# Attention message passing on one core: two tiles for the drained product bank, earlier spreading scans, and a later second widening

## The reference

```python
def _egat_layer(nf, ef, src, dst, W_ni, W_nj, W_fij, W_node, attn, bias):
    f_out = nf @ W_ni [src] + nf @ W_nj [dst] + ef @ W_fij + bias
    f_out = leaky_relu(f_out, 0.2).reshape(-1, H, D)
    e = einsum('ehd,hd->eh', f_out, attn)
    a = exp(e - segment_max(e, dst)[dst])
    a = a / segment_sum(a, dst)[dst]
    h = (nf @ W_node).reshape(-1, H, D)
    return segment_sum(h[src] * a[:, :, None], dst), f_out
for l in range(3):
    nfh, efh = _egat_layer(nf, ef, src, dst, ...)
    nf, ef = nfh.mean(axis=1), efh.mean(axis=1)
return x + nf
```

## Time and profile before

| | |
|---|---|
| median of 2 runs | 3717.05 us (3715.75 to 3718.35) |
| the profiled execution | 3716.28 us, its span 3714.5 us |
| TensorE busy | 2692.3 us, 72% |
| VectorE busy | 2424.4 us, 65% |
| GpSimd busy | 1891.6 us, 51% |
| ScalarE busy | 1634.7 us, 44% |
| mean granted TensorE clock | 0.777 of 2.4 GHz |

### The profile page before, as it was taken

How to read it: one execution, slowest core, us unless ns; L and a number is a source line. 1 busy time by engine, 2 the same in 40 slices (tenths; PEclk the granted TensorE clock), 3 DMA queues, 4 the chain that set the end, 5 groups by cost and what they waited for, 6 DMA issues and landing times.

```text
span 3714.5 us, 54737 instructions
## 1 busy us (share of the span) xinstructions
PE 2692.3 (72%) x18232; PEld 2153.1 (58%) x18259; DVE 2424.4 (65%) x5843; ACT 1634.7 (44%) x4133; POOL 1891.6 (51%) x1987
## 2 busy tenths in 40 slices
PE   3477777768677458777777777856777787777885
PEld 2465656656565256566666656536666666666653
DVE  6376767767768536676676767753667576676775
ACT  0144544544445315454454545532444444444453
POOL 5544554554553266455554545446555454554543
PEclk8787777777879778787777878868777777777776
DMA  6244334434342334343434433233343333433322
GB/s 218 86 122 137 120 122 144 128 126 133 122 130 88 121 107 119 115 137 114 147 120 134 126 115 122 98 107 110 100 121 119 112 108 105 123 114 114 95 81 84
DMA packets 149064, 440.48 MB, mean 119 GB/s; under 512 B 40892, under 2 KB 80672, under 8 KB 129977
## 3 DMA queue, kind: packets, MB, share of 16 engines
q1 hardware_dynamic: 82746, 385.31, 29.4%
q0 software_dynamic: 63200, 36.75, 7.1%
q10 hardware_dynamic: 2838, 14.91, 1.0%
HBM read 191.89 MB, written 244.95 MB: 118 GB/s over the span
## 4 chain that ended last, share of the span: by engine, by line
DVE 36%; PE 36%; issue 13%; ACT 9%; DMA 4%; POOL 2%; DVEq 0%; ACTq 0%; SPq 0%; POOLq 0%
DVE U L1465 15%; PE pick_ps L732 14%; PE f_ps L764 11%; PE f_ps L773 5%; DVE U L1450 4%; ACT f_low L919 4%; DVE rows L1386 4%; PE xT_ps L754 4%; DVE lr L1397 4%; DVE rows L1491 3%; ACT xT L910 2%; DMA z<-hot_tab 1%; ACT pick_sb L973 1%; DVE z L1477 1%; DVE mx_sc L1421 1%
## 5 line engine op out<-in xcount | busy, mean ns | idle before, releaser
L615 POOL DMA_INDIRECT rows<-nf_tab,src_sb x1815 | 1721.8, 949 | 1505.0 <-PE xT_ps L754 669.6
L732 PE MATMUL pick_ps<-nf_part,z 125*128 125x160 bf16 x9045 | 926.1, 270 | 578.9 <-ACT pick_sb L973 446.4
L732 PEld LDWEIGHTS pick_ps<-nf_part,z 125*128 125x128 bf16 x9045 | 835.1, 115 | 624.4 <-issue 459.9
L1397 DVE TENSOR_TENSOR lr<-f_ps,f_low 128x512 f32<-128x512 f32 x606 | 413.3, 682 | 930.7 <-ACT f_low L919 930.5
L773 PEld LDWEIGHTS f_ps<-w_out,lr 128*128 128x128 f32 x4836 | 721.4, 215 | 396.4 <-issue 296.7
L764 PE MATMUL f_ps<-xT,w_edge 97*128 97x512 f32 x1212 | 804.5, 752 | 70.2 <-ACT ef_new L941 47.2
L1465 DVE TENSOR_TENSOR_SCAN U<-wide_ps,U 128x272 f32<-128x272 f32 (+2 forms) x1272 | 801.9, 694 | 3.0 <-ACT wide_ps L982 1.9
L773 PE MATMUL f_ps<-w_out,lr 128*128 128x36 f32 (+1 forms) x4836 | 663.7, 278 | 30.2 <-DVE lr L1397 27.8
L919 ACT ACTIVATE f_low<-f_ps 128x512 f32<-128x512 f32 x606 | 360.6, 595 | 652.8 <-PE f_ps L764 652.5
L754 PE MATMUL xT_ps<-ident,rows 128*97 128x128 f32 x2418 | 449.9, 314 | 170.9 <-DVE rows L1386 141.8
L754 PEld LDWEIGHTS xT_ps<-ident,rows 128*97 128x97 f32 x2418 | 330.0, 186 | 188.5 <-DVE rows L1386 146.9
(11 more groups left out here) (164 smaller groups left out, 1215.4 us busy)
## 6 DMA issues: line engine op xcount, KB each, us to landing
u_tab<-up SPq DMA_DIRECT2D x144, 1088.0 KB, 5.0
z<-hot_tab SPq DMA_DIRECT2D x134, 468.8 KB
s_nd<-edge_first SPq DMA_DIRECT2D x48, 768.0 KB, 7.1
hot_tab<-z SPq DMA_DIRECT2D x67, 468.8 KB
rows<-nf_tab,src_sb POOLq DMA_INDIRECT x1815, 3.5
ef_tab<-ef_new SPq DMA_DIRECT2D x32, 768.0 KB, 4.1
ef_st<-ef_tab SPq DMA_DIRECT2D x32, 768.0 KB
edge_first<-s_nd ACTq DMA_DIRECT2D x16, 768.0 KB, 11.3
```

What stands on the lines that cost most here:

```text
L615: eng.indirect_dma_start(rows[q % RING][:, c * K:c * K + D], None, nf_tab[:, :], bass.IndirectOffsetOnAxis(ap=src_sb[:, t:t + 1], axis=0)) ...
L732: mm = eng.matmul(pick_ps[:, i * PB:(i + 1) * PB], hot[m % HOTS][0:NQ, f * PW + i * P:f * PW + (i + 1) * P], nf_part[a][0:NQ, f * PB:(f + ...
L1397: eng.tensor_tensor(lr[y][:, 0:w], f_ps[n % 2][:, 0:w], f_low[y][:, 0:w], ALU.max).then_inc(lr_ready, 1)
```

## The change

It has three parts. `rest4` becomes two views, of `m_spread` and `jw`, which take turns by batch, and the copy into one waits for the picks of the batch two before; `pick_sb` goes away. The scans of `spread_dst` are dealt out over nine slots instead of ten, so that the last ones stand in slot 8. In the loop `widen(k, 3)` moves from ahead of `take_xT` and `lower` to behind `lower`.

```diff
-SPREAD0 = (2, 5, 3, 3, 2, 5, 3, 3, 2, 4)
-SPREAD = (4, 4, 3, 2, 4, 4, 2, 2, 4, 3)
+SPREAD0 = (2, 5, 3, 3, 3, 5, 4, 4, 3)
+SPREAD = (4, 4, 3, 3, 4, 4, 3, 3, 4)
...
-        pick_sb = sb("pick_sb", [P, PICK * (PB - D)])
-        rest4 = pick_sb[:, :].rearrange("p (c b d) -> p c b d", b=PARTS5 - 1, d=D)
+        rest4 = [a[:, 0:PICK * (PB - D)].rearrange("p (c b d) -> p c b d", b=PARTS5 - 1, d=D)
+                 for a in (m_spread, jw)]
...
-                        if m:
-                            eng.wait_ge(picked, (PARTS5 - 1) * m)
-                        eng.activation(rest4, pick4[:, :, 1:PARTS5, :], ACT.Copy
+                        if m >= 2:
+                            eng.wait_ge(picked, (PARTS5 - 1) * (m - 1))
+                        eng.activation(rest4[m % 2], pick4[:, :, 1:PARTS5, :], ACT.Copy
                                        ).then_inc(drained, 1)
...
                         if mine and i == 3:
                             widen(k, 2)
-                            widen(k, 3)
                         take_xT(g + 2)
                         if g + 1 >= 0:
                             lower(g + 1)
+                        if mine and i == 3:
+                            widen(k, 3)
...
-                                rest4[:, :, v - 1, :]).then_inc(picked, 1)
+                                rest4[m % 2][:, :, v - 1, :]).then_inc(picked, 1)
```

## The result

| | before | after |
|---|---|---|
| median of 2 runs | 3717.05 us | 3026.73 us (3024.26 to 3029.19) |
| ratio, 95% interval | | 0.8145, 0.8126 to 0.8165 |
| span of the profiled execution | 3714.5 us | 3027.4 us |
| TensorE busy | 2692.3 us, 72% | 2429.6 us, 80% |
| VectorE busy | 2424.4 us, 65% | 2404.9 us, 79% |

The changed kernel is faster, by 690 us; the prediction had 3045 us. VectorE does nearly the same work in 687 us less span. All of that lies in the three main loops: from `leaky` of group 0 to `leaky` of group 182 they take 821, 705 and 736 us, 2262 together, against 995, 964 and 989, 2948 together; the tails are as long as before.

A forecast was written before the change was run, and what follows sets the result against it. No engine was full; three stalls in slots 8 to 0 left VectorE half idle for a third of each supergroup. Saving 48.1 us per supergroup over three layers, 14 times, 673 us, gave 3045 us; range 2940 to 3260 us.

The forecast's parts named there:

- A: Slot 8: ScalarE's product-bank copy waits for VectorE's picks of the batch before; 4.44 us of VectorE idle time, to go.
- C: Slots 11 and 0: the same copy wait, with picks after `leaky` and four scans; VectorE idle 5.28 us, to go.
- the first rival: One stall half kept, where copies, pick and edges follow each other: 176 us less gained, about 3220 us; chance 0.15.
- Spreading: Scans end in slot 8, so the next supergroup's transposes find them done; some tenths of a us stay in slot 9.
- The later widening: Slots 3, 7 and 11: ScalarE lowers the next group about 1.3 us sooner; the moved instruction costs nothing.
- Pauses and the clock: Remaining TensorE pauses, like 1.74 us in slot 5, cost 0 to 3 us per supergroup; 1.5 us taken.
- the walk: Three queues followed through slots 8 to 11: waits of 0.2, 0.15, 0.35 us; layer 1 supergroup 44.9 us without pauses.
- the sum: Savings per supergroup of 9.8, 18.3 and 20.0 us in layers 0, 1, 2, together 48.1; 14 times is 673 us.
- The clock rival: Many short pauses keep TensorE at 1.2 GHz half the time, setting layers 1 and 2's pace: 3404 us; chance 0.10.
- Layer 0: Slot 8's wait for one-hot tiles stays: VectorE idle 4 us, then 2 us in slot 9; supergroup 57.25 us.
- GpSimd: Rival: gathers, 44 us a supergroup, become the bound; a tenth slower means 56 us less gained, 3100 us; chance 0.06.
- B: Slot 9: TensorE's transposes of the next supergroup wait for VectorE's scans behind the product; about 5.3 us VectorE idle.

The follow-up runs named there:

- The filled kernel: The changed kernel plus TensorE products that nobody reads, in its pauses in slots 6 and 9 and ahead of slot 10's transposes: 2964.56 us, ratio 0.7969.

## Why the prediction was right, point by point

*Where the time lies.* Right. The gain lies in the main loops, which lost 686 of the 687 us of span, and in the slots of the three stalls.

*Two tiles.* Right for A and C together with the other parts: slots 9 and 0 of layer 1 show no wait. The later link in C that the first rival feared, copies, pick and `edges` at half clock, does not stand: 0.00, 0.00 and 0.33 us in slot 0.

*Spreading.* Half right. The step said that the transposes find the scans done. They do not always: 31 waits remain, 1.51 us in the one shown, because TensorE is ahead of VectorE's scans of slot 8. This is the first step that failed. It is small in itself, but most of what layer 2 lost against the forecast stands behind this pause (see the pauses below).

*The later widening.* Right: slot 3 is at 0.00 in every layer, slot 7 at 0.16 to 0.65 us, and nothing waits for the moved instruction in a way that the waits show.

*Pauses and the clock.* The term that was mis-sized. I took 1.5 us per supergroup in every layer. The filled kernel shows the walk with the clock at 1.00: 44.99 us in layer 1, where the sum had 44.9. Against it the pauses cost 46.66 - 44.99 = 1.67 us in layer 1 and 49.05 - 45.27 = 3.78 us in layer 2. Of this, slots 0 to 7 have 0.78 and 0.77 us, and slots 8 to 11 have 0.90 and 3.00 us. So layer 1 came out at 46.66 us (46.4 said), layer 2 at 49.05 (46.6 said). My 1.5 us was the middle of what two supergroups showed in slots 0 to 7; I had no term for a pause ahead of the transposes, where the two layers differ. And the supergroup that I read for layer 1 is its better kind: in the kernel before, slots 0 to 7 of layer 1 take 31.7 us at 1.00 and 34.6 us at 0.88 in turn, 33.01 us on the mean, and slot 5 has a clock of 0.65 in six of thirteen supergroups after the same pause of 1.74 us.

*The clock rival.* Its mechanism is there, at about a quarter of my price: the fillings, which change only what TensorE does in its pauses, win back 84 us in the loops, where the rival had TensorE set the pace in two layers and lose 673 - 312 = 361 us against the sum. In the kernel with the one-hot tiles in slot 7, where layer 0 can be filled too, filling wins 105 us in the loops. What I held against this rival, layer 1 at 1.00, was true of the supergroup read and not of the layer. The Trainium skill, "TensorE: Matmul & The Clock Gate", section "A second HAM failure mode: psum-queue depth-cycling", says that frequent small idle times make the clock go back and forth. The supergroup of layer 2 shown, with 0.66 in slots 8 to 11 after a pause of 1.51 us, agrees with it, and so does the 1.00 once the pauses are filled.

*Layer 0.* Right in kind: the wait for the one-hot tiles stays, 4.05 us (4 said), and slot 10 has 1.58 us (2 said); moving the tiles took the first away. The period is 54.86 us, not 57.25: VectorE's work is 48.03 us on the mean (48.75 said), and other waits and pauses come to 54.86 - 48.03 - 4.05 - 1.58 = 1.20 us where I had 2.5.

*The sum.* Saved per supergroup: 12.2 + 18.0 + 17.5 = 47.7 us, 48.1 said. Layer 0 did 2.4 us better and layer 2 2.5 us worse, so the closeness of the total owes something to luck. The factor was 14; the loops' 686 us are 14.4 times 47.7, because the supergroups at both ends of a loop gain as well. Time: 3026.73 us, 3045 said.

*GpSimd.* Right that it does not bind: it still waits 145.4 us for TensorE, and a load of 46.1 us left the time as it was.

*What I said would show it.* ScalarE's wait vanished; TensorE's did not, it fell to a quarter. `leaky`'s wait is below 400 us, but layer 0 holds only the largest part of it (in the loops 96, 47 and 77 us), not most. The clock in slots 8 to 11 of layer 1 is 0.81 in the supergroup first shown, below the 0.9 I named, but 0.93 over thirteen supergroups; layer 2 has 0.81 there. Of the signs of being wrong one shows in part: `leaky` waits 3.06 us in slot 11 in five of thirteen supergroups of layer 2, where the longest before was 2.32 us; the mean, 1.90 us, is that of before (1.92).

*What the sum hid.* I added A, B and C as if each had its price by itself. In the whole change that comes out, since all three go. For one part alone it would not have: the tiles alone leave B whole, and the scans alone win half of B. Of the 690 us about 110 belong to no single part. They come with the scans: scans and tiles together bring 0.024 of the time more than the two singly, scans and widening 0.036 more, tiles and widening nothing more (0.1227 against 0.1283).

## What to carry to other kernels

Where several stalls follow each other in one period, list what each engine finds when the stall in front of it is gone; a single edit moves the waiting to the next link, and its price alone says little of its price in the whole. After the long waits look for the short ones: a pause of 1.5 us ahead of TensorE can cost more in the two steps behind it, at half clock, than it lasts, and products that nobody reads can buy that back where TensorE has time to spare. Give each layer its own term where their rows differ, and read several periods of a layer before one of them stands for it: here two kinds took turns. Where parts may depend on each other, run them in pairs too; the pair without the tiles showed that the tiles were not the only reason for the higher price of the scans.

## What the runs showed of the hardware

- In the changed kernel TensorE pauses 1.88 us ahead of the pick of slot 6 in every supergroup of layer 1 that was read; behind it the clock fell in five of thirteen and stayed at 1.00 in eight. A pause of 1.26 us ahead of the transposes of step 10 was followed by 1.00 in some and by the lower clock in others. The mean clock in slot 9, behind the scans, is 0.84 in layer 1 and 0.75 in layer 2. What decides was not settled.
- Products in such pauses kept the granted clock at 1.00 in slots 8 to 11 of layers 1 and 2 and were worth 1.67 and 3.78 us of periods of 46.66 and 49.05 us, though TensorE had more to do.
- A memset of 168 ns on GpSimd behind each gather cost 44 ns a gather: the idle time ahead of the next gather fell from 0.29 to 0.16 us.
